# One ring of four PSUM banks, four-step turns, a convolution in four 64x64 tiles and u's whole difference on GpSimd, in the first stage of a normalise, convolve and filter kernel

## What is computed

```python
c  = (x - mean_c(x)) / sqrt(var_c(x) + 1e-6)          # over the 64 channels
x1 = x + c + batchnorm(conv3x3(sign(c), sign(w) * mean|w|))
t  = tokens(x1)                                        # 3136 tokens x 64 channels per image
u  = (t - mean(t)) / sqrt(var(t) + 1e-5)
# t + a weighted sum of four long filters of u over the first 3136, 1568, 784, 392 tokens
```

## Time and profile before

| | us |
|---|---|
| median of 3 runs (1602.16 to 1607.21) | 1603.73 |
| profiled execution, its own time | 1594.29 |
| its span, first to last instruction | 1592.6 |
| PE busy, matmuls / weight loads | 1309.8 / 906.4 |
| DVE, ACT, POOL busy | 994.5, 828.9, 502.2 |
| mean granted TensorE clock (1.0 is 2.4 GHz) | 0.918 |

### The profile page before, as it was taken

One profiled execution on the slowest core, in us unless ns is written; L12 is line 12 of the kernel. 1 busy time (PEld: TensorE's weight loads), 2 busy tenths in 40 slices (PEclk: granted clock), 3 DMA queues, 4 the chain that ended last, 5 costly groups with the idle time before them and its releaser, 6 DMA issues. The chain is left out here.

```text
span 1592.6 us, 34784 instructions
## 1 busy us (share of the span) xinstructions
PE 1309.8 (82%) x13633; PEld 906.4 (57%) x13633; DVE 994.5 (62%) x1404; ACT 828.9 (52%) x1455; POOL 502.2 (32%) x441
## 2 busy tenths in 40 slices
PE   1888888888888888846989999999999991967757
PEld 1444444444444444412869899889899880433323
DVE  5287777767767776777647777667777760523324
ACT  0866666666666666225546556556556550222212
POOL 2135555555555555540022232222232232000000
PEclk9999999999999999968989999999999995978878
DMA  6022444444444442743499998889889876988883
GB/s 204 1 81 87 131 131 134 134 134 134 134 134 134 134 134 94 150 148 116 141 294 276 272 271 269 253 252 260 247 265 274 250 220 233 372 324 320 338 338 152
DMA packets 179612, 317.40 MB, mean 199 GB/s; under 512 B 14805, under 2 KB 154423, under 8 KB 162935
## 3 DMA queue, kind: packets, MB, share of 16 engines
q1 hardware_dynamic: 164966, 257.40, 52.0%
q0 software_dynamic: 14592, 59.26, 10.2%
HBM read 162.86 MB, written 153.76 MB: 199 GB/s over the span
## 5 line engine op out<-in xcount | busy, mean ns | idle before, releaser
L969 POOL DMA_DIRECT2D w_scratch<-wf x256 | 151.2, 594 | 454.0 <-ACT y_sb L1147 418.8
L522 PE MATMUL p_conv<-signs_padded,conv_w 128*128 128x448 bf16 x1008 | 232.4, 380 | 23.9 <-DVE x_all L701 23.9
L1028 PE MATMUL ring<-v_mov,m_sta 105*128 105x128 f16 x4096 | 234.1, 219 | 0.5 <-issue 0.5
L1028 PEld LDWEIGHTS ring<-v_mov,m_sta 105*128 105x128 f16 x4096 | 231.5, 98 | 1.0 <-issue 0.6
L551 PE MATMUL p_xt<-u_t,step_masked 98*128 98x512 f32 x256 | 148.8, 712 | 79.5 <-ACT z_sb L603 71.1
L456 POOL TENSOR_TENSOR u_t<-u_t,root 98x1024 f32<-98x1024 f32 x62 | 118.1, 1937 | 291.7 <-DVE root L745 291.7
L1164 DVE COPY hf<-ring 128x512 f32<-128x512 f32 x256 | 168.7, 689 | 27.5 <-PE ring L1028 26.5
L1147 ACT ACTIVATE hf<-ring 128x512 f32<-128x512 f32 x256 | 152.9, 597 | 59.5 <-PE ring L1028 57.6
L522 PEld LDWEIGHTS p_conv<-signs_padded,conv_w 128*128 128x128 bf16 x1008 | 101.8, 103 | 142.4 <-issue 74.5
L1297 PE MATMUL p_out<-w_in,last_masked 128*98 128x512 f32 x256 | 142.9, 643 | 23.8 <-DMA w_in<-w_scratch 23.8
L1353 ACT ACTIVATE out_sb<-p_turn 128x392 f32<-128x392 f32 x128 | 62.6, 498 | 191.7 <-PE p_turn L1309 177.4
(11 more groups left out here) (133 smaller groups left out, 1986.5 us busy)
## 6 DMA issues: line engine op xcount, KB each, us to landing
z_in<-z_scratch SPq DMA_DIRECT2D x32, 1076.5 KB, 8.3
z_scratch<-z_sb SPq DMA_DIRECT2D x16, 2048.0 KB, 8.9
y_scratch<-y_sb SPq DMA_DIRECT2D x32, 1024.0 KB, 9.0
yt<-y_scratch SPq DMA_DIRECT2D x64, 512.0 KB, 6.4
w_scratch<-wf POOLq DMA_DIRECT2D x256, 128.0 KB, 5.3
w_in<-w_scratch SPq DMA_DIRECT2D x8, 4096.0 KB, 14.9
x_all<-in_x SPq DMA_DIRECT2D x16, 1568.0 KB, 7.5
x_scratch<-x_t SPq DMA_DIRECT2D x16, 1568.0 KB
```

The costliest lines, as they stand in the source:

```text
L522: mm = nc.tensor.matmul(p_conv[:, g % 2, 0:CW], keep["conv_w"][:, t, :], pad[q % 2][:, rows, t % 3:t % 3 + WID], start=(t == 0), stop=(t = ...
L969: nc.gpsimd.dma_start(w_units[u, h, s, c], wf[64 * c:64 * c + 64, 2 * h + s].rearrange("p (g n) -> p g n", n=256)).then_inc(w_stored, 16)
L1028: mm = nc.tensor.matmul(bank[:, 2 * NF * i:2 * NF * i + 2 * NF], m_sta[:, 2 * e + 1 - n:2 * e + 3 - n, :].rearrange("k b d -> k (b d)"), v ...
```

## The change

The seven chunks of 8 rows become four steps j of 7 rows, for the upper and the lower half of the image at once (h = 0, 1). The signs of the lower half are stored with the two images swapped, and a second 128x128 block of the centring constant gives that swap. Each tap of a step is four 64x64 matmuls at four tile positions, two into bank h = 0 and two into bank h = 1. A pair now has 12 centring chunks: kind 0 gives the swapped lower half (signs alone, 29 rows), kind 1 the upper half and one row (copy and signs, 29 rows), kind 2 the rest (copy alone, 27 rows). `turn_x`, `step1` and `center` share one ring of four banks; the convolution and `turn_r` share the other four. The transform, `copy_x` and `save_z` are spread over the four steps, the bias goes behind the signs, the square root behind the eighth centring chunk. POOL forms all four quarters of u's difference, and `center_u` is gone from DVE.

```diff
+HROWS = HGT // 2
+CROWS = 7
-    center = np.kron(np.eye(2), np.eye(CH) - 1.0 / CH)
+    center = np.kron(np.hstack([np.eye(2), np.eye(2)[::-1]]), np.eye(CH) - 1.0 / CH)
...
+        ring = own.enter_context(nc.psum_tensor("ring_norm", [128, RING1, 512], F32))
+        p_conv = own.enter_context(nc.psum_tensor("p_conv", [128, 4, 512], F32))
...
+        at, count = {}, 0
+        for it in TURNS:
+            for j in range(4):
+                for c in (2 * j, 2 * j + 1):
+                    if there(it + 1):
+                        at["x", it + 1, c], count = count, count + 1
+                for c in (2 * j, 2 * j + 1):
+                    if there(it - 2):
+                        at["z", it - 2, c], count = count, count + 1
+            for c in range(NCEN):
+                if there(it + 2):
+                    at["cen", it + 2, c], count = count, count + 1
...
+            def bank_free(*chunk):
+                if at[chunk] >= RING1:
+                    pe.wait_ge(freed, at[chunk] - RING1 + 1)
+            def convolve(q, j):
+                if j == 0:
+                    pe.wait_ge(freed, until("cen", q, NCEN - 1))
+                    if there(q - 1):
+                        pe.wait_ge(r_done, NCONV * (q - 1) + 6)
+                elif j == 1:
+                    if there(q - 1):
+                        pe.wait_ge(x1_done, NTOK * (q - 1) + NTOK)
+                else:
+                    pe.wait_ge(r_done, NCONV * q + 2 * j - 2)
+                bank = p_conv[:, 2 * (j % 2):2 * (j % 2) + 2, :]
                 for t in range(9):
+                    rows = slice(CROWS * j + t // 3, CROWS * j + t // 3 + CROWS)
+                    for h in range(2):
+                        for k in range(2):
+                            out = k if h == 0 else 1 - k
+                            mm = nc.tensor.matmul(bank[CH * out:CH * out + CH, h, 0:CW],
+                                                  keep["conv_w"][CH * k:CH * k + CH, t, CH * k:CH * k + CH],
+                                                  pad[q % 2][CH * k:CH * k + CH, h, rows, t % 3:t % 3 + WID],
+                                                  start=(t == 0), stop=(t == 8), tile_position=(CH * k, CH * out))
+                        if t == 8:
+                            mm.then_inc(conv_ready, 1)
...
             for it in TURNS:
+                for j in range(4):
                     if there(it):
+                        convolve(it, j)
+                    for c in (2 * j, 2 * j + 1):
+                        if there(it + 1):
+                            turn_x(it + 1, c)
+                    for c in (2 * j, 2 * j + 1):
+                        if there(it - 2):
+                            step1(it - 2, c)
+                if there(it + 2):
+                    for c in range(NCEN - NSIGN):
+                        center(it + 2, c)
                 for c in range(NTOK):
                     if there(it):
                         turn_r(it, c)
+                    if c % 2 == 0 and there(it + 2) and NCEN - NSIGN + c // 2 < NCEN:
+                        center(it + 2, NCEN - NSIGN + c // 2)
...
@@ scalar
+                for j in range(4):
+                    for c in (2 * j, 2 * j + 1):
+                        if there(it + 1):
+                            copy_x(it + 1, c)
+                    for c in (2 * j, 2 * j + 1):
+                        if there(it - 2):
+                            save_z(it - 2, c)
+                    if j >= 2 and there(it - 1):
+                        square2(it - 1, j - 2)
+                for c in range(NCEN):
+                    if there(it + 2):
+                        signs(it + 2, c)
+                    if c == 7 and (there(it + 1) or there(it - 1)):
+                        square_root(it)
                 if there(it + 1):
                     add_bias(it + 1)
...
@@ gpsimd
-                    for c in (2, 3):
+                    for c in range(4):
                         v = slice(2 * c, 2 * c + 2)
                         nc.gpsimd.tensor_tensor(u_t[q % 2][:, v, :].rearrange(groups, n=CH),
...
-                                                ALU.subtract).then_inc(u_centered_late, 1)
+                                                ALU.subtract).then_inc(u_centered, 1)
```

More of the change, by code:

```diff
@@ L446, in x_of, with centred, bank_of, until @@
             return x_all[:, TOK * (q % 3):TOK * (q % 3) + TOK]
+        def centred(k):
+            i, kind = divmod(k, 3)
+            first = SROWS * i
+            if kind == 1:
+                return 0, first, min(SROWS, HROWS + 1 - first)
+            if kind == 0:
+                return 1, HROWS - 1 + first, min(SROWS, HROWS + 1 - first)
+            return 0, HROWS + 1 + first, min(SROWS, HROWS - 1 - first)
+        at, count = {}, 0
[10 more added lines that the diff above has]
+                    at["cen", it + 2, c], count = count, count + 1
+        def bank_of(*chunk):
+            return ring[:, at[chunk] % RING1, :]
+        def until(*chunk):
+            return at[chunk] + 1
         def roots_of(it):
@@ L501, in turn_x @@
                 if c == 0:
[L502 to L507, removed]
+                    pe.wait_ge(freed, until("cen", q, NCEN - 1))
+                bank_free("x", q, c)
                 for j in range(ACH):
@@ L538, in step1 @@
             def step1(q, c):
-                if c >= 2 or not there(q + 3):
-                    if NTOK * q + c >= 2:
-                        pe.wait_ge(z_saved, NTOK * q + c - 1)
-                else:
-                    pe.wait_ge(xt_copied, NTOK * (q + 3) + NTOK - 1 + c)
-                    pe.wait_ge(xt_squared, NTOK * (q + 3) + NTOK - 1 + c)
+                bank_free("z", q, c)
                 if c % 2 == 0:
@@ L626, in _ @@
             for it in TURNS:
-                if there(it + 1):
-                    for c in range(NTOK):
-                        copy_x(it + 1, c)
-                if there(it - 1):
-                    for h in range(2):
-                        square2(it - 1, h)
+                for j in range(4):
[12 more added lines that the diff above has]
+                        square_root(it)
                 if there(it + 1):
                     add_bias(it + 1)
-                if there(it - 2):
-                    for c in range(NTOK):
-                        save_z(it - 2, c)
-                for c in range(NCONV):
-                    if there(it + 2):
-                        signs(it + 2, c)
-                    if c == 1 and (there(it + 1) or there(it - 1)):
-                        square_root(it)
         @block.gpsimd
```

138 lines of the change are left out of this document (56 added, 82 removed).

## The result

| | before | after |
|---|---|---|
| median of the runs | 1602.95 (4 runs, 1599.99 to 1607.21) | 1476.63 (4 runs, 1474.78 to 1481.71) |
| ratio, 95% interval | | 0.9215 [0.9184, 0.9247] |
| profiled execution, own time / span | 1594.29 / 1592.6 | 1481.71 / 1479.9 |
| mean granted clock of that execution | 0.918 | 0.93 |

The medians lie 126.3 us apart, forecast 134.3: the changed kernel came out 7.6 us above the forecast of 1469, inside the range.

A forecast was written before the change was run, and what follows sets the result against it. The order of the lists (ACT, then PE at half clock), no engine's sum, was taken as the bound. Gains of 105.5, 9.4, 17.6 and 1.8 make 134.3 off 1594.3; 1460.0 plus 9.4 gives 1469 us, range 1447 to 1535.

The forecast's parts named there:

- Part 1: PE's convolution: four tiled steps of 1.7 us, 6.8 per turn in place of 12.0, a gain of 5.2.
- B: Rival: tiles of two row positions don't overlap in one bank; 3.15 us per step, 1528 us in all; chance 0.14.
- C: Rival: the four tiles run one by one; 6.1 us per step, 1708 us in all; chance 0.05.
- Part 3: u's difference: DVE loses 3.44 us, POOL forms all pieces at 1.9 us each; POOL's 22.6 per turn no bound.
- E: Rival: POOL's difference stays at 2.9 us a piece, +1.2 a turn, 1484 us; within the forecast's own range, no separate chance.
- Part 4: The new middle turn followed through the engines, waits included: 31.7 us in place of 40.5.
- p: Time in us within a turn, counted from PE's start of step 0.
- T: Instant when the previous turn's reciprocal root is done and POOL's turn begins; forecast at p 1.5, the next at 33.2.
- D: Rival: the clock still falls once per turn, at the signs' wait or in step 0; +41, 1510 us; chance 0.12.
- Turns 14 to 16: The stage's late turns: 29.3 + 26.0 + 22.3 = 77.6 us in place of 95.2, a gain of 17.6.
- The forecast's own terms: Up to turn 2: more centring +1.6, bias no longer ahead of signs -2.8, turn 0 -3, turn 1 27.2 for 32.
- The last turn: Stage end: z's store goes out earlier than before, PE's eight slow `step1` bound the turn; a gain of 1.8 us.

The follow-up runs named there:

- e1: The changed kernel with the convolution untiled, each tap one 128x128 matmul per half of the image: 1534.05 us, ratio 0.9608 to before.
- e2: The changed kernel with DVE forming the first half of u's difference again, POOL the second: 1474.73 us, ratio 0.9243 to before.
- e3: The kernel before, with only POOL forming all four quarters of u's difference and DVE none: 1617.69 us, ratio 1.0137 to before.
- e5: The changed kernel with ACT's second square moved behind the second chunk of signs: 1470.61 us, ratio 0.9205 to before.
- e6: e5 with `sums2(0)` also put ahead of `sums1(1)` on DVE: 1468.57 us, ratio 0.9191 to before.
- run 36: Not a follow-up run: "run" is the verb here, four tiles run the 36 bf16 matmuls of one convolution step, in 1.64 us.
- e9: e6 with one unused bf16 matmul before each float32 pair of the block that combines the filter matrices: 1467.14 us, ratio 0.9195 to before.
- e11: e9 run again unchanged, beside a repeat of e6: 1473.76 us, ratio 0.9177 to before.

## Why the forecast held, and where it was off

- **Part 1.** A step's convolution was priced at 1.7, with the 0.2 for the change of tiling in it. It took 1.64 and another 0.17 around it, 1.81 in all, so a whole step is 4.40 instead of 4.3. The nearly full overlap of four tiles, with two row positions in a bank, holds; rivals B (3.15) and C (6.1) fall by the same lines. e1 gives the tiling's share, 57 us.
- **Part 3.** A piece takes 1.87 (forecast 1.9; E's 2.9 falls), and e2 confirms that this part is off the path. e3 shows what moves where that cover is missing, the second square, 1.7 us later.
- **Part 4, the turn.** Counted as in the forecast from PE's step 0 (276.57 for the turn read above, 308.47 less 31.9): steps end at p 18.3 (forecast 18.4; step 0 was 0.35 shorter and the other three together 0.2 longer than forecast, so their sum is closer than its terms), the second square ends at 21.3 (21.3), the fifth centre waits 0.52 (0.5), eight centres are done at 25.2 (25.1), T stands at 33.1 (33.2). The turn is 31.9, not 31.7, only because T lies 1.2 us behind PE's step 0, not 1.5 as before. The wait in step 0 was 0.50, not 1.2: T came 0.3 earlier, and from T to the first `step1` it was 2.05 us, not 2.3. The clock is 1.00 in the middle turns: D falls there. Twelve turns: 2.8 us less gain than forecast.
- **Near miss inside it.** The sums of squares and the variance were said to end at 24.3. They end at 302.37, p 25.8, and the first `add_r` starts at 25.9: DVE was 0.1 us from holding it up. e5 and e6 show that a little more would still have cost nothing: in e5 the first `add_r` starts right at the variance's end, 0.1 later in the turn than in e6, and the turns are equally long. The step that failed left out that `sums1(1)`, which waits for ACT's last copies, stands ahead of both `sums2`.
- **Turns 14 to 16**, the mis-sized term: 81.6 us instead of 77.6. Turn 14 took 32.5 for a forecast 29.3. Without centring to do, PE reaches the first `add_r` early, and there those three sums of DVE hold it, a wait of 7.16 us; then it transposes at half clock, five groups in 4.98 us:

```profile
526.66 4.98 PE L582 MATMUL p_conv<-ident,x_all 128*98 128x128 f32 x20 [7.16 <-DVE x_t L797]
```

  e6 takes 1.7 of it back by the order of the sums alone. Turn 15 was 27.9 for 26.0, turn 16 21.2 for 22.3.
- **Outer ends.** T of turn 2 moved by -8.9 (-9.4). The forecast's own terms, +1.6 - 2.8 - 3 - 4.8, give -9.0. Read at PE's first convolution of each turn they were -1.9 ahead of turn 0 (67.62 to 65.72) for a forecast -1.2, -2.2 in turn 0 for -3, and -4.5 in turn 1 for -4.8; the rest is the 0.3 by which T lies closer: part of the agreement is luck. The last turn gave 4.4, not 1.8: `step1` was priced as slow all through, but the clock was back at 1.00 from 591 us on, and its sixteen records took 9.36 us. The store of z lands in 8.9 us, and no instruction in the middle turns waits for it, as said.
- **The scale.** The sum was made on the profiled execution, 9.4 below the median of the runs shown, and that distance was added, without a cause for it. The profiled execution of before turned out to be one with the block at full clock, that of the change one at half: between these two the miss is 21.7 us (1481.7 for 1460.0), of which 17 lie outside the stage. By medians, the miss is 8.0 of 134.3; by the start of the second stage it is 4.7, and the last 3.3 are within what executions differ by. No term of the forecast spoke of that block: that the miss by medians is so much the smaller one is in part luck.

## What to carry over

Read a software-pipelined stage as the interval of one event per turn, and follow one turn engine by engine in list order; the sum of PE's work gave 28.8 us, and the chain that includes the waits 31.7, of a measured 31.9. Do the same for the first and last turns, where another engine's list decides because the work that hid it is missing. And compare a block that a change doesn't touch in both traces before putting a difference down to it: here 10 us hung on the clock that a block ran at, which differed between executions of one kernel.

## What the runs showed of the hardware

- Four 64x64 tiles, two row positions into each of two banks, run 36 bf16 matmuls of 392 columns in 1.64 us, 0.18 per tap for all four (one untiled matmul of 392 columns costs 0.168 in e1, 3.02/18); with a bank per row position it is 1.64, too.
- Going from untiled float32 matmuls into tiled bf16 ones and out again costs 0.17 us, 0.09 on the way in and 0.08 on the way out (1.81 against 1.72, 0.95 against 0.87), seen as longer spacings and not as idle time: PE is busy for 30.43 of 31.90 us, and the waits of 0.50, 0.52 and 0.44 are the rest.
- DVE's difference (98x2048, float32, two inputs) and POOL's two-input instructions (98x1024) don't overlap: whichever starts second waits for the other. POOL's first piece took 3.9 us instead of 1.87 in e2, DVE's 2.88 and 3.44 instead of 2.15 (the last number worked out from these).
- A block of float32 matmuls in which PE is busy without a break (31.5 us) stayed at 1.2 GHz to its end in one execution (0.51 and 0.50 in its windows), and ran at 1.00 in another. With a bf16 matmul in front of each pair it was the same: 1.00 in e9's profiled execution (16.60 us of 16.60 busy), 0.50 in e11's (15.46 of 15.46).
